# GNN layers: edges sorted on chip by target block, counts within the edge loop, target rows by one-hot products

## The chip, the cores and the metric

One core of one Trainium2 chip runs the whole program. The metric is device microseconds of one execution; the profile is of one further execution. Engines are named as in the profile: PE (TensorE), DVE (VectorE), ACT (ScalarE), POOL (GpSimd) and SP (SyncE).

## The reference, cut to what matters

625 nodes of 768 features, 20000 edges (src, dst). The reference is four blocks of a graph layer and a feed-forward or mixture layer. The part that changes is the first graph block, twice:

```python
fs = (x @ Ws + bs).reshape(-1, H, D)
fd = (x @ Wd + bd).reshape(-1, H, D)
e = jax.nn.leaky_relu(fs[src] + fd[dst], 0.2)
logits = jnp.einsum('ehd,hd->eh', e, attn)
m = jax.ops.segment_max(logits, dst, num_segments=N)
ex = jnp.exp(logits - m[dst])
denom = jax.ops.segment_sum(ex, dst, num_segments=N)
alpha = ex / denom[dst]
out = jax.ops.segment_sum(alpha[:, :, None] * fs[src], dst, num_segments=N)
```

H is 8 in the first layer and 1 in the second. A logit depends only on the pair (dst, src), so the kernel keeps a 625 x 625 table of logits and a 625 x 625 matrix of edge counts C, and forms the softmax densely with the logarithm of the counts added.

## The kernel before

The program is written by hand, engine by engine, with counted semaphores; each engine's order is that of its block of code. Stages are: layer norm and two linear layers (`linear`), first edge loop, attention over the table (`attend(0)`), two linear layers, second edge loop, `attend(1)`, then a mixture of 8 experts in units of up to 256 tokens (`mixture0`), and the later layers.

Nodes are split into T = 5 blocks of R = 125, edges into ET = 157 tiles of 128. The linear layers write rows of 776 floats (768 features, 8 linear terms), source rows by way of `F` to `src_rows`, target rows by way of `O` to `dst_rows` in DRAM (`edge_rows`, SP's `in_two`).

First edge loop, per tile: POOL issues an indirect gather of 128 source rows (L562) and of 128 target rows (L565) into one of EU = 8 buffer pairs, and six tiles later the indirect scatter of the 8 logits (L578), which waits for `s_lg` and for the landing of the scatter before. ACT copies each half of the target rows into PSUM (L1028); DVE adds the half of the source rows (L1377) and multiplies the positive part by the attention vector (L1379); then come the small sum of the linear terms (L1384), the sums per head (L1388) and the logit (L1412). Beside this the counts are built: DVE makes the one-hot of the targets (L1329, 626 columns, bf16 from fp16), ACT that of the sources (L1032, L1037), and PE adds their product into seven PSUM banks, eleven products a tile (L647, `count`).

Second edge loop, per tile: the same DMAs, scattering one logit into two tables in turn; ACT copies whole target rows into PSUM (L1048), DVE adds (L1393) and takes the whole product with its sum (L1397), then L1412. PE has no work. The loops of PE, ACT and DVE are `Fori` loops of eight tiles; POOL's is written out. `mixture0` is a `Fori` over at most NU = 12 units with an `If` inside; 8 units run, and PE reads a number of empty eighths (L875) and branches to one of five variants in each.

At the start SP loads x, then constants, then the edges; ACT's queue fills the logit tables (`zero_logits`).

## Time and profile before

| what | us |
|---|---|
| runs of the kernel | 3960.14, 3953.3, 3954.85 (median 3954.85) |
| the profiled execution, its own time | 3953.68 |
| its span, first to last instruction | 3951.8 |
| busy: PE / DVE / ACT / POOL | 2386.9 / 2330.5 / 1365.2 / 1002.3 |
| mean granted clock of PE | 0.770 of 2.4 GHz |

Busy time of an engine leaves out register, branch, semaphore and DMA-issuing instructions. A four-byte matmul has two records on PE. "Issue" as a releaser means that an engine waited for nothing the profile shows, "remote" that the release has no record.

### The profile page before, as it was taken

The numbers are of one execution on the slowest core, as the hardware profiler recorded it, in microseconds if no ns is written. First come the engines' busy times: TensorE is split into PE (matmuls) and PEld (weight loads), VectorE is DVE, ScalarE is ACT, GpSimd is POOL, SyncE is SP. The second block draws the span as 40 slices with busy tenths as digits, with TensorE's granted clock in tenths as the row PEclk, the third lists the DMA queues.
The fourth block names the chain that finished last, engine by engine and source line by source line (L and its number), as shares of the span: only waits on it lengthen the run. The fifth ranks groups of instructions, "written<-read, shape, count | busy, mean of one in ns | idle before, by whom it ended". The sixth has DMA issues, their size and how long they took to land.

```text
span 3951.8 us, 39567 instructions
## 1 busy us (share of the span) xinstructions
PE 2386.9 (60%) x12372; PEld 1922.0 (49%) x12373; DVE 2330.5 (59%) x4711; ACT 1365.2 (35%) x2102; POOL 1002.3 (25%) x1052
## 2 busy tenths in 40 slices
PE   8454455556700000034598988886788588797899
PEld 4243333345400000013588888775375345477798
DVE  4687777787344444435787776665575623576332
ACT  0455555554011111111465555553171101144110
POOL 0566666630176666631100000001000000000000
PEclk9766766677855555565799998988789698898899
DMA  9656565657376666630676555554200001100211
GB/s 283 186 168 181 169 175 173 175 167 280 97 193 187 191 190 189 187 103 1 221 252 204 204 200 186 184 181 149 80 1 12 21 17 37 60 13 25 72 72 43
DMA packets 118376, 546.25 MB, mean 138 GB/s; under 512 B 31254, under 2 KB 31510, under 8 KB 112904
## 3 DMA queue, kind: packets, MB, share of 16 engines
q0 software_dynamic: 69520, 283.95, 24.6%
q1 hardware_dynamic: 47142, 244.22, 18.5%
q10 hardware_dynamic: 1540, 15.63, 1.3%
q8 instruction: 126, 2.06, 0.2%
q14 instruction: 48, 0.39, 0.0%
HBM read 487.87 MB, written 55.82 MB: 138 GB/s over the span
## 4 chain that ended last, share of the span: by engine, by line
PE 43%; DVE 22%; issue 14%; POOL 7%; DMA 6%; ACT 4%; another core or an unknown queue 3%; DVEq 1%; SPq 0%; POOLq 0%; ACTq 0%
PE PS L678 10%; PE PS L931 6%; PE PS L830 5%; PE PS L733 5%; PE PS L845 4%; DVE PS L1377 4%; DVE WB L1379 3%; POOL WB L562 2%; PE PS L832 2%; POOL WB L565 2%; PE PS L848 2%; DVE WB L1397 2%; DVE W L1478 1%; PE PS L719 1%
## 5 line engine op out<-in xcount | busy, mean ns | idle before, releaser
L647 PE MATMUL PS<-O 128*125 128x512 bf16 (+9 forms) x1727 | 378.1, 390 | 355.7 <-ACT O L1037 260.4
L719 PE MATMUL PS<-ident,W 125*125 125x125 f32 x650 | 114.1, 313 | 747.8 <-issue 684.5
L647 PEld LDWEIGHTS PS<-O 128*125 128x125 bf16 x1727 | 261.6, 191 | 472.3 <-issue 306.1
L719 PEld LDWEIGHTS PS<-ident,W 125*125 125x125 f32 x650 | 95.4, 214 | 764.4 <-issue 706.1
L830 PE MATMUL PS<-urowsT,w1s 128*128 128x384 f32 (+4 forms) x1164 | 365.9, 382 | 94.1 <-issue 73.3
L678 PE MATMUL PS<-WB,XT 128*125 128x384 f32 (+1 forms) x1120 | 385.2, 507 | 31.9 <-DMA WB<-in_L_gnn_W 17.0
L562 POOL DMA_INDIRECT WB<-src_rows,idx x314 | 304.8, 971 | 288.4 <-DMA dst_rows<-O 193.3
L845 PE MATMUL PS<-hid,w2s 128*128 128x384 f32 (+3 forms) x1152 | 326.4, 357 | 0.5 <-DVE hid L1727 0.5
L678 PEld LDWEIGHTS PS<-WB,XT 128*125 128x125 f32 x1120 | 214.1, 192 | 200.0 <-issue 36.8
L733 PE MATMUL PS<-F,PT 125*125 125x96 f32 (+3 forms) x1500 | 292.6, 348 | 17.8 <-ACT PT L1103 8.2
L1048 ACT COPY PS<-WB 128x776 f32<-128x776 f32 x138 | 111.6, 809 | 551.5 <-DVE lgr L1412 367.9
L832 PE MATMUL PS<-urowsT,w1s 128*128 128x192 f32 (+4 forms) x1164 | 301.1, 259 | 0.0
L578 POOL DMA_INDIRECT logits<-lgr,key x236 | 233.9, 991 | 230.4 <-DVE lgr L1412 142.7
L550 POOL TENSOR_TENSOR rstd<-var,mhalf 125x1 f32<-125x1 f32 x50 | 41.5, 831 | 987.2 <-DVE var L1302 987.2
L830 PEld LDWEIGHTS PS<-urowsT,w1s 128*128 128x128 f32 x1164 | 233.6, 201 | 111.2 <-issue 91.2
L565 POOL DMA_INDIRECT WB<-dst_rows,idx x276 | 261.4, 947 | 85.2 <-issue 83.7
L848 PE MATMUL PS<-hid,w2s 128*128 128x192 f32 (+3 forms) x1152 | 282.3, 245 | 0.0
L1393 DVE TENSOR_TENSOR PS<-WB,PS 128x776 f32<-128x776 f32 x157 | 152.4, 971 | 219.9 <-ACT PS L1048 129.9
L931 PE MATMUL PS<-w3s,XT 128*128 128x384 f32 x1440 | 254.7, 339 | 11.1 <-DVE w3s L1792 11.1
L931 PEld LDWEIGHTS PS<-w3s,XT 128*128 128x128 f32 x1440 | 254.4, 189 | 12.3 <-issue 12.2
L733 PEld LDWEIGHTS PS<-F,PT 125*125 125x125 f32 x1500 | 230.5, 202 | 60.1 <-issue 17.2
L832 PEld LDWEIGHTS PS<-urowsT,w1s 128*128 128x128 f32 x1164 | 237.3, 204 | 0.0
(251 smaller groups left out, 4809.7 us busy)
## 6 DMA issues: line engine op xcount, KB each, us to landing
XN<-in_L_ffn_w SPq DMA_DIRECT2D x98, 769.0 KB, 4.4
PB<-in_L_ffn_w SPq DMA_DIRECT2D x97, 768.0 KB, 5.6
logits<-NEG ACTq DMA_DIRECT2D x8, 1367.2 KB
WB<-logits SPq DMA_DIRECT2D x5, 2187.5 KB
slot_rows<-WB POOLq DMA_DIRECT2D x13, 768.0 KB, 29.6
slot_outs<-WB POOLq DMA_DIRECT2D x12, 768.0 KB, 54.5
C<-in_L_ffn_expert_w SPq DMA_DIRECT2D x8, 1152.0 KB, 5.6
NEG<-in_L_ffn_expert_w SPq DMA_DIRECT2D x8, 1152.0 KB, 6.8
```

Source lines behind the costliest of these rows:

```text
L562: pool.indirect_dma_start(out=gs[u], out_offset=None, in_=src_rows, in_offset=bass.IndirectOffsetOnAxis(ap=idx[:, i, 0:1], axis=0)).then_i ...
L565: pool.indirect_dma_start(out=gd[u], out_offset=None, in_=dst_rows, in_offset=bass.IndirectOffsetOnAxis(ap=idx[:, i, 1:2], axis=0)).then_i ...
L578: pool.indirect_dma_start(out=table, out_offset=bass.IndirectOffsetOnAxis(ap=key[:, i:i + 1], axis=0), in_=lgr[:, i % EU, 0:HEADS[g]["h"]] ...
L647: mm = pe.matmul(PSz[0:R, a:b], oh[:, slot, 1, c * R:(c + 1) * R], oh[:, slot, 0, a - c * N:b - c * N], start=(first and fresh), stop=last ...
L678: mm = pe.matmul(PS[0:R, 4 + g % 4, 0:hw], XT[:, k, t * R:(t + 1) * R], w[:, k, half * hw:(half + 1) * hw], start=(k == 0), stop=(k == kc ...
L719: tr = pe.transpose(PSz[0:R, 1024 * (1 + s % 2) + b * P:1024 * (1 + s % 2) + b * P + R], src[:, b * R:(b + 1) * R], ident[0:R, 0:R])
L733: mm = pe.matmul(PS[0:R, bank, 0:cw], PT[0:R, s % 2, b, :], F[0:R, b, col:col + cw], start=(b == 0), stop=(b == T - 1))
L830: pe.matmul(both(q % 2, columns), w1s[:, g % 2, 0, w:w + P], urowsT2[:, :, k * TU:k * TU + columns], start=k == 0, stop=False)
L832: mm = pe.matmul(PS[:, q % 2, 0:columns], w1s[:, g % 2, 1, w:w + P], urowsT2[:, 0, k * TU:k * TU + columns], start=False, stop=k == KD - 1)
L845: pe.matmul(both(2 + k, columns), w2s[:, g % 2, 0, w:w + P], hid2[:, g % 2, :, c * TU:c * TU + columns], start=g == 0 and c == 0, stop=False)
L848: mm = pe.matmul(PS[:, 2 + k, 0:columns], w2s[:, g % 2, 1, w:w + P], hid2[:, g % 2, 0, c * TU:c * TU + columns], start=False, stop=g == NG ...
L931: mm = pe.matmul(PS[:, 4 + 2 * ((MB3 + d) % 2) + half, 0:384], XT2[:, a, k, t * R:t * R + P], w3s[:, 2 * u + k // 3, b, col:col + 384], st ...
```

## The change

- Ahead of the first layer norm DVE counts, for each edge, its place in an order by target block (`rank_edges`: comparisons, a prefix sum in eight steps, two small products on PE for the sums over partitions). Each block starts a new tile, so there are ES = 161 tiles, the rest padded.
- The edges are moved on PE between the pieces of the two linear layers (`move_edges`): the product of a one-hot of the place within a tile (ACT, `place_onehots`) and of the place's tile times the node numbers (DVE, `edge_values`), in groups of NB = 16.
- All edges of a tile now have targets in one block. Their target rows are no longer gathered from DRAM: PE multiplies the turned one-hot of the targets (128 edges from 125 nodes) with that block's rows in `O` and adds to source rows that ACT copied into PSUM. `dst_rows` and its writes are gone. The turned one-hots come from the target numbers, turned once, stored to DRAM and spread over all partitions by DMA in chunks of 16 tiles (`spread_targets`).
- A tile's counts touch one block: two products in place of eleven, banks 0 to 4 and the last 113 columns in banks 5 and 6. The long one-hot is made by DVE for even tiles, by ACT for odd ones. PE reads the tile's block number into a register (`block`).
- The second loop uses the same sum on PE. All edge loops and the units of `mixture0` are written out instead of `Fori`.
- Edges, iota and ident are loaded ahead of x; the table fills go to SP's queue; POOL does the two large memsets.

```diff
+ES = (E + T * (P - 1)) // P
+NB = 16
...
-        zh = PS[:, 7, 0:D // 2]
-        zw = [PSz[:, 1024 * b:1024 * b + GW] for b in range(4)]
+        zw = [PS[:, 2 * b:2 * b + 2, 0:GW // 2] for b in range(4)]
+        zA = PS[:, 6, P - 15:P - 15 + HA]
+        zB = PS[:, 7, 0:GW - HA]
+        rest = PSz[0:R, 5 * 512:5 * 512 + T * P].rearrange("p (c n) -> p c n", c=T)[:, :, 0:N - 512]
...
+            def spread_targets(g):
+                chunks = -(-ES // CH)
+                sp.wait_ge(s_frow, 2 * T * (g + 1))
+                for c in range(chunks):
+                    q = g * chunks + c
+                    if c >= 2:
+                        sp.wait_ge(s_tt, ES * g + CH * (c - 1))
+                    a, b = CH * c, min(CH * (c + 1), ES)
+                    sp.dma_start(spread_ids[q % 2][:, 0:(b - a) * P],
+                                 targets[a:b].rearrange("(o t) p -> o (t p)", o=1).to_broadcast([P, (b - a) * P]))\
+                      .then_inc(s_idb[q % 2], 16)
...
-                pool.indirect_dma_start(
-                    out=gd[u], out_offset=None, in_=dst_rows,
-                    in_offset=bass.IndirectOffsetOnAxis(ap=idx[:, i, 1:2], axis=0)).then_inc(s_gat[u], 16)
+                    in_offset=bass.IndirectOffsetOnAxis(ap=source[:, i:i + 1], axis=0)).then_inc(s_gat[u], 16)
...
+            def move_edges(a, b):
+                pe.wait_ge(s_trc, 2 * T)
+                for t in range(a, min(b, ET)):
+                    pe.wait_ge(s_q, t + 1)
+                    pe.wait_ge(s_val, t + 1)
+                    pe.matmul(PS[:, 0, 0:2 * ES], ohq[t % NB], ohv[t % NB], start=t == 0, stop=t == ET - 1)\
+                      .then_inc(s_pm, 1)
...
+            def first_edges():
+                pe.wait_ge(s_line, 2 * T * 2)
+                pe.wait_ge(s_zero, 1)
+                for bank in (2, 3, 4, 5, 6, 7, 0, 1):
+                    if bank == 1:
+                        pe.wait_ge(s_idc, 1)
+                    mm = pe.matmul(PS[:, bank, :], NEG[:, 0, 0:P], iota[:, 0:512], start=True, stop=False,
+                                   skip_group_check=True)
+                mm.then_inc(s_seed, 1)
+                pe.wait_ge(s_frow, 2 * T)
+                c, then = block(0), block(1)
+                for i in range(ES):
+                    wait(pe, s_wa, i)
+                    pe.wait_ge(s_oh, i + 1)
+                    if i % 2:
+                        pe.wait_ge(s_ohs, i // 2 + 1)
+                    pe.matmul(rest[:, bass.ds(c, 1), :].rearrange("p o n -> p (o n)"), oht[i % 4][:, 0:R],
+                              ohs[i % 4][:, 512:N], start=False, stop=i == ES - 1, skip_group_check=True)\
+                      .then_inc(s_rem, 1)
+                    pe.matmul(PS[0:R, bass.ds(c, 1), :].rearrange("p o n -> p (o n)"), oht[i % 4][:, 0:R],
+                              ohs[i % 4][:, 0:512], start=False, stop=i == ES - 1, skip_group_check=True)\
+                      .then_inc(s_ohu, 1)
+                    pe.wait_ge(s_tt, i + 1)
+                    pe.wait_ge(s_ca, i + 1)
+                    pe.matmul(zA, ohT[i % 2], O[0:R, bass.ds(c, 1), 0:HA].rearrange("p o n -> p (o n)"),
+                              start=False, stop=True, skip_group_check=True).then_inc(s_za, 1)
+                    pe.wait_ge(s_gc, i + 1)
+                    pe.matmul(zB, ohT[i % 2], O[0:R, bass.ds(c, 1), HA:GW].rearrange("p o n -> p (o n)"),
+                              start=False, stop=True, skip_group_check=True).then_inc(s_zp, 1)
+                    c, then = then, block(i + 2) if i + 2 < ES else None
...
+            linear(0, lambda t: move_edges(NB * (t - 1), NB * t) if t else None)
+            linear(1, lambda t: move_edges(NB * (T + t - 1), NB * (T + t)))
+            move_edges(NB * (2 * T - 1), ET)
+            turn_targets()
+            first_edges()
...
-                with pe.Fori(1, NU) as u:
-                    with pe.If(u < units):
+                for u in range(1, NU):
+                    with pe.If(units > u):
...
+            def place_onehots(a, b):
+                def place_gap(t):
+                    wait(act, s_q, t - 1)
+                    act.activation(qgap[t % 2], iota16[:, 0:P], ACT.Abs, bias=place_in[:, t:t + 1], scale=-1.0)\
+                       .then_inc(s_qg, 1)
+                if a == 0:
+                    act.wait_ge(s_place, 1)
+                    place_gap(0)
+                for t in range(a, b):
+                    if t + 1 < ET:
+                        place_gap(t + 1)
+                    act.wait_ge(s_qg, t + 1)
+                    wait(act, s_pm, t - NB + 1)
+                    act.activation(ohq[t % NB], qgap[t % 2], ACT.Relu, bias=ones[:, 0:1], scale=-1.0).then_inc(s_q, 1)
...
+            def edge_values(a, b):
+                for t in range(a, min(b, ET)):
+                    wait(dve, s_pm, t - NB + 1)
+                    dve.tensor_scalar(ohv[t % NB][:, 0:ES], iota16[:, 0:ES], tile_of[:, t:t + 1], dst1[:, t:t + 1],
+                                      ALU.is_equal, ALU.mult)
+                    dve.tensor_scalar(ohv[t % NB][:, ES:2 * ES], iota16[:, 0:ES], tile_of[:, t:t + 1],
+                                      src1[:, t:t + 1], ALU.is_equal, ALU.mult).then_inc(s_val, 1)
...
+                for i in range(2):
+                    count_onehots(i)
+                    turned_onehot(0, i)
+                for i in range(ES):
+                    weigh_first(i)
+                    if i:
+                        head_sums(i - 1)
+                    if i + 2 < ES:
+                        count_onehots(i + 2)
+                    weigh_last(i)
+                    if i + 2 < ES:
+                        turned_onehot(0, i + 2)
+                    if i:
+                        finish(i - 1)
...
+            pool.memset(NEG[:], 0.0).then_inc(s_zero, 1)
+            pool.memset(C[:], NEGBIG).then_inc(s_low, 1)
```

The order on DVE, first edge loop, one tile before (`gs`, `gd` and the products are in WB, PS is PSUM, PB holds the attention vector):

```order
L1377 TENSOR_TENSOR PS<-WB,PS 128x384
L1379 SCALAR_TENSOR_TENSOR WB<-PS,PB 128x384
L1329 TENSOR_SCALAR O<-XT,idf 128x626
L1377 TENSOR_TENSOR PS<-WB,PS 128x384
L1379 SCALAR_TENSOR_TENSOR WB<-PS,PB 128x384
L1384 TENSOR_TENSOR WB<-WB 128x8
L1388 TENSOR_REDUCE dots<-WB 128x8
L1412 SCALAR_TENSOR_TENSOR lgr<-dots,WB 128x8
```

and now, for a tile in which the long one-hot is DVE's:

```order
L1633 SCALAR_TENSOR_TENSOR WB<-PS,WB 128x392
L1646 TENSOR_REDUCE dots<-WB 128x8
L1573 TENSOR_SCALAR O<-XT,idf 128x125
L1575 TENSOR_SCALAR W<-XT,idf 128x626
L1639 COPY F<-PS 128x8
L1640 SCALAR_TENSOR_TENSOR WB<-PS,WB 128x384
L1625 TENSOR_SCALAR WB<-WB,node 125x128
L1653 SCALAR_TENSOR_TENSOR lgr<-dots,F 128x8
```

The two additions are gone; the short one-hot, the tail copy and the turned one-hot are new; the long one-hot is in every second tile.

The order on PE, first edge loop, one tile now (before it was eleven L647 products of 53 to 512 columns and nothing else):

```order
L747 TENSOR_LOAD idx
L747 ISA x2
L766 ISA
L766 MATMUL PS<-W,O 125x113
L769 ISA
L769 MATMUL PS<-W,O 125x512
L774 ISA
L774 MATMUL PS<-O,WB 128x392
L777 ISA
L777 MATMUL PS<-O,WB 128x384
```

Counts first, then the two four-byte products of the target rows; the rows ISA and TENSOR_LOAD set registers.

The order on PE in the linear layers, before:

```order
L662 MATMUL PS<-ident,XN 128x125 x30
L678 MATMUL PS<-WB,XT 125x384 x120
```

and now, one of its nine rounds:

```order
L827 MATMUL PS<-WB,XT 125x384 x12
L737 MATMUL PS<-W,O 128x322 x9
L737 MATMUL PS<-PT,O 128x322 x6
L737 MATMUL PS<-PT,F 128x322
```

After each twelve products of a linear layer (from the second on) sixteen tiles of edges are moved.

## Rows read from the trace of the kernel before

**Rows 1.** Engines by stage: PE, PEld, DVE, ACT, POOL busy us, clock, DMA.

```profile
0.00:108.00 108.00, 84.77 (x270) 51.17 (x271) 46.72 (x78) 6.02 (x11) 4.25 (x9) 1.00 0.87 266
108.00:840.00 732.00, 378.07 (x1727) 261.64 (x1727) 556.69 (x1258) 390.57 (x629) 456.40 (x471) 0.67 0.59 171
...
1068.00:1727.00 659.00, 0.00 (x0) 0.00 (x0) 313.15 (x628) 127.02 (x157) 455.64 (x470) 0.50 0.67 189
```

**Rows 2.** First edge loop, groups by form: out<-in, shapes xcount | busy us, mean ns | idle.

```profile
L1377 DVE TENSOR_TENSOR PS<-WB,PS 128x384 f32<-128x384 f32 x310 | 172.9, 558 | 26.2 <-issue 13.5 <-ACT PS L1028 12.2
L1379 DVE SCALAR_TENSOR_TENSOR WB<-PS,PB 128x384 f32<-128x384 f32 x310 | 172.7, 557 | 10.7
L578 POOL DMA_INDIRECT logits<-lgr,key x154 | 152.1, 988 | 170.3 <-DVE lgr L1412 99.3 <-issue 63.7 <-DMA logits<-lgr,key 7.3
L562 POOL DMA_INDIRECT WB<-src_rows,idx x152 | 147.5, 971 | 46.3 <-issue 46.3
L1388 DVE TENSOR_REDUCE dots<-WB 128x8 f32<-128x768 f32 x154 | 146.8, 953 | 0.0
L1028 ACT COPY PS<-WB 128x384 f32<-128x384 f32 x271 | 130.8, 483 | 193.8 <-DVE WB L1379 148.6 <-issue 45.2
L565 POOL DMA_INDIRECT WB<-dst_rows,idx x134 | 127.0, 947 | 41.9 <-issue 40.4 <-DMA logits<-lgr,key 1.5
L1037 ACT ACTIVATE O<-XT,ones 128x626 bf16<-128x626 bf16 x155 | 126.1, 814 | 104.7 <-remote 99.7 <-PE PS L647 5.0
...
L1329 DVE TENSOR_SCALAR O<-XT,idf 128x626 bf16<-128x626 f16 x155 | 61.2, 395 | 128.2 <-remote 118.5 <-PE PS L647 9.4
...
L1412 DVE SCALAR_TENSOR_TENSOR lgr<-dots,WB 128x8 f32<-128x8 f32 x154 | 24.2, 157 | 0.0
```

**Rows 3.** First edge loop, in order of time: start us, us, what [idle before <-releaser].

```profile
553.40 0.39 DVE L1329 TENSOR_SCALAR O<-XT,idf 128x626 bf16<-128x626 f16 x1 [4.69 <-remote]
...
554.31 2.91 PE L647 MATMUL PS<-O 128*125 128x512 bf16 x11 [6.45 <-ACT O L1037]
...
562.21 1.56 PE L647 MATMUL PS<-O 128*125 128x512 bf16 x11 [0.93 <-ACT O L1037]
```

**Rows 4.** Waits of the first edge loop: us in total, times, longest us.

```profile
DVE O L1329 <- remote: 118.5, 33, 6.3
```

**Rows 5.** Second edge loop, groups by form, columns as in rows 2.

```profile
L1393 DVE TENSOR_TENSOR PS<-WB,PS 128x776 f32<-128x776 f32 x147 | 142.7, 971 | 202.8 <-ACT PS L1048 114.0 <-issue 88.8
L562 POOL DMA_INDIRECT WB<-src_rows,idx x147 | 142.6, 970 | 44.8 <-issue 44.8
L1397 DVE SCALAR_TENSOR_TENSOR WB<-PS,PB 128x768 f32<-128x768 f32 x147 | 139.9, 952 | 6.5 <-DVE PS L1393 5.4 <-issue 1.1
```

**Rows 6.** First and last start of one line in each loop.

```profile
L1377 DVE TENSOR_TENSOR PS<-WB,PS x314: 543/555/564, 116.1 to 832.7; 128x384 f32<-128x384 f32 x157
...
L1393 DVE TENSOR_TENSOR PS<-WB,PS x157: 970/971/972, 1073.8 to 1718.8; 128x776 f32<-128x776 f32 x157
```

**Rows 7.** Start of the program, in order of time, columns as in rows 3.

```profile
12.18 1.02 DVE L1299 BATCH_NORM_STATS2 stats<-X 125x6 f32<-125x384 f32 x2 [4.49 <-DMA X<-in_x]
...
24.69 77.97 PE L678 MATMUL PS<-WB,XT 128*125 128x384 f32 x240
...
108.27 1.19 POOL L562 DMA_INDIRECT WB<-src_rows,idx  x1 [86.82 <-DMA dst_rows<-O]
```

**Rows 8.** A short activation, group by form on ACT, whole span.

```profile
L1155 ACT ACTIVATE F<-F 128x256 f32<-128x256 f32 x192 | 77.7, 415 | 51.2 <-DVE F L1717 50.0
```

**Rows 9.** DMA issues of the page: KB each, median us to landing.

```profile
XN<-in_L_ffn_w SPq DMA_DIRECT2D x98, 769.0 KB, 4.4
```

**Rows 10.** Seams of mixture units on PE, in order of time, columns as in rows 3.

```profile
2104.85 0.68 PE L830 MATMUL PS<-urowsT,w1s 128*128 128x384 f32 x1 [10.81 <-issue]
...
2202.19 0.74 PE L830 MATMUL PS<-urowsT,w1s 128*128 128x448 f32 x1 [5.80 <-issue]
```

**Rows 11.** Waits of PE from unit 1 to the last, columns as in rows 4.

```profile
PE PS L830 <- issue: 71.9, 6, 16.3
```

More of the change, by code:

```diff
@@ L623, in _ @@
             unit_store(0)
-            with pool.Fori(1, NU) as u:
-                with pool.If(u < units):
+            for u in range(1, NU):
+                with pool.If(units > u):
                     unit_store(u)
@@ new lines, in second_edges @@
+            def second_edges():
+                pe.wait_ge(s_line, 2 * T * 4)
+                for bank in range(8):
+                    mm = pe.matmul(PS[:, bank, 0:GW // 2], ones[:], iota[:, 0:GW // 2], start=True, stop=False,
+                                   skip_group_check=True)
+                mm.then_inc(s_seed, 1)
+                pe.wait_ge(s_frow, 4 * T)
+                c, then = block(0), block(1)
+                for i in range(ES):
+                    pe.wait_ge(s_tt, ES + i + 1)
+                    pe.wait_ge(s_gc, ES + i + 1)
+                    for half in range(2):
+                        mm = pe.matmul(zw[i % 4][:, half, :], ohT[i % 2],
+                                       O[0:R, bass.ds(c, 1), half * (GW // 2):(half + 1) * (GW // 2)]
+                                       .rearrange("p o n -> p (o n)"), start=False, stop=True, skip_group_check=True)
+                    mm.then_inc(s_zp, 1)
+                    c, then = then, block(i + 2) if i + 2 < ES else None
@@ L680, in linear @@
                         mm.then_inc(s_linp, 1)
-            def count_edges():
-                for i in range(EU):
-                    count(i, i % 2, first=i == 0)
-                with pe.Fori(1, ER) as j:
-                    for u in range(EU):
-                        count(j * EU + u, u % 2)
-                for i in range(ER * EU, ET):
-                    count(i, i % 2, last=i == ET - 1)
-                pe.wait_ge(s_cnt, 1)
+                    if between:
+                        between(t)
             def attend(n):
@@ L1187, in mixture0 @@
                 unit(0)
-                with act.Fori(1, NU) as u:
-                    with act.If(u < units):
+                for u in range(1, NU):
+                    with act.If(units > u):
                         unit(u)
@@ L1764, in mixture0 @@
                 unit(0)
-                with dve.Fori(1, NU) as u:
-                    with dve.If(u < units):
+                for u in range(1, NU):
+                    with dve.If(units > u):
                         unit(u)
```

519 lines of the change are left out of this document (323 added, 196 removed).

## The prediction

> **What bounds the kernel now.** I read the stages first, then the groups of the two edge loops, then waits and order of time where these left a question.
>
> The two edge loops last 732 and 659 us of the 3951.8 us span, over a third [rows 1]. In the first, DVE is busy 557 us and POOL 456 us, PE's mean clock is 0.67 of full; in the second PE does nothing at all. The reader should see that POOL's busy time hides a gap after each of its DMAs: "issue" before the 152 source gathers is 46.3 us, 0.30 us each [rows 2]. With it a first-loop tile costs POOL 0.97 + 0.95 + 0.99 + 3 x 0.30 = 3.81 us. DVE spends 2 x 0.558 + 2 x 0.557 + 0.953 + 0.395 and two small operations of 0.157 = 3.89 us, partly overlapped [rows 2]. Undisturbed tiles follow each other every 3.83 us: DVE and POOL bind together. The stage is longer, because DVE waits 33 times, 118.5 us in all, at its one-hot for a release no record explains [rows 4]. Such a stall is at 553.40: DVE and PE stop together, PE resumes at half clock (2.91 us for a tile's eleven count products) and is back at full (1.56 us) two tiles later [rows 3]. I can't name its cause, only that PE ran at full clock with idle time in each tile before it. From first to last product the loop takes 116.1 to 832.7, the second 1073.8 to 1718.8 [rows 6]: 717 and 645 us, 4.6 and 4.1 us per step.
>
> **The change, part by part.**
>
> Front. The sort stands ahead of the layer norm on DVE: some 75 operations. From the two forms of 384 and 776 columns (0.558 and 0.971 us [rows 2, 5]) an operation costs 0.153 us + 1.07 ns per column; about 11,000 columns and 75 starts give 23 us, and 17 if the two-byte ones run at double rate, as L1329 does (626 columns in 0.395 us). I take 20. It starts when edges, iota and ident have landed, now ahead of x. X was there at 12.18 [rows 7]; I take 6, so the places are ready at 26. Then ACT makes 16 place one-hots before it copies transposed rows. An activation of 128 columns is, by the line through 0.415 us for 256 and 0.814 us for 626 [rows 2, 8], 0.28 us, so a pair is 0.57 us and the sixteen 9 us. Ten copies of about 0.6 us follow: the linears start at 42 in place of 24.69 [rows 7]. Their 240 records take 78 us. Between them PE moves 157 tiles; a count product averages 284 columns in 1.56/11 = 0.14 us [rows 3], so 322 columns are about 0.18 us, 28 us on PE's path. ACT needs 16 x 0.57 = 9.1 us per batch against PE's 7.8 + 2.9, DVE 16 x 2 x 0.24 = 7.7 us beside some 3 us of row work: both just hidden; were PE faster, ACT would be next. The linears and moves end at 148, sorted_edges (nine short operations) at 152. The old first gather, at 108.27, waited for dst_rows [rows 7]; that wait goes. In its place comes a chain: turn on PE, copy on ACT, store, spread, one-hot. A DMA of 769 KB lands in 4.4 us [rows 9]; two in a row are 4 to 9 us, I take 7, with PE and ACT 9. PE's eight opening products of 512 columns, 8 x 0.87 = 7 us, lie beside that chain (before the second loop 5 us beside its first gather). SP's 20 table fills moved ahead of the row stores, and POOL's two memsets ahead of its roots: both have over 100 and 15 us of cover; without it the tables (15.6 MB) would hold the source rows back by tens of us. First product at 161 for 116.1: **+45 us**, between +25 and +75.
>
> First loop, DVE: products of 392 and 384 columns 0.566 + 0.557; head sums 0.953; short one-hot 0.14 (125 columns, by L1329's rate); the long one every second tile 0.20; tail copy 0.12 to 0.157; turned one-hot of 128 columns, two-byte in, four-byte out, 0.14 to 0.29, taken 0.20; finish 0.157. Sum 2.9 us. POOL: one gather and one scatter, 0.97 + 0.99 + 0.60 = 2.56 us. ACT: 2 x 0.49, and 1.63/2 = 1.8 us. PE, at full clock: a four-byte product of 384 columns is two records of 0.325 us [rows 7], so 0.66 + 0.65, counts 0.27, and up to 0.2 for weights not loaded ahead, since each product stands behind a wait: about 2.0 us. The chain that closes through PE: rest product, ACT's copy, first 392 columns, DVE's first product; with 0.05 to 0.15 us per handover 2.4 us at full clock, shorter than DVE's. At half clock PE's own order decides: 1.5 + 1.4 (the two products) + 0.3 (rest) + 0.65 (ACT's copy and handovers) = 3.9 us. So 3.0 at full, 3.9 at half. The old loop's mean of 0.67 [rows 1] means full clock for a third of its time; PE will be busy for two thirds of a tile at full clock where it was for 1.56 of 3.83 us, so I choose 70% at full, between a third and all: 3.25 us. 161 x 3.25 = 523 for 717: **-194 us**. Reading the block number into a PE register and four computed addresses per tile cost, by no row here, anything from nothing (PE's sequencer works ahead) up to the 5.80 us of a seam [rows 10]; each mixture unit reads one too, and of the seven seams only six have a gap [rows 11], so I take nothing and keep the upper end for a rival.
>
> Second loop: DVE 0.97 (weigh, add moved to PE) + 0.08 + 0.20 + 0.157 = 1.4 us, ACT 0.81, POOL 2.56, PE 1.3 to 1.5 us at full and 2.7 to 2.9 at half clock. POOL's 2.56 and a PE that drifts between clocks give 2.6 to 2.9; the old loop ran 8% over POOL's 3.81; I take 2.75, 443 for 645: **-202 us**. Its start gains about 6 us: the gather no longer waits for the target rows to land, though SP's spread takes part of that place. **-6 us**.
>
> Mixture units. The loop over units becomes straight code. At six seams PE idles 71.9 us on "issue" [rows 11]: the shortest, 5.80, I read as the jump back, the longer (10.81 to 16.3) as that and jumps into a column variant [rows 10]. The latter stay. 6 x 5.8 = 35 us go; four skipped units now are far jumps on DVE ahead of the last gathers, 4 x 5.8 less what POOL's last store hides, about 10 us. **-25 us**, between 0 and -60. The Trainium skill, Runtime: NRT & Kernel Launch, "Instruction fetch mechanics", says that a taken branch out of the current window must fetch its target before going on. By that rule even the skipped units cost a fetch each; the gaps of 5.80 and 10.81 us agree with it.
>
> Sum: 45 - 194 - 202 - 6 - 25 = -382. Against the profiled execution's own 3953.7 us that is 3571; attend(1) finds PE warm and its first sums (idle PE before) some 2 us faster. I say **3570 us**. The median of the runs shown lies 1.2 us above that execution: no difference here.
>
> A rule against the change. L562 gathers take 0.971 us in the first loop, where DVE runs its two-byte one-hot at double rate, and 0.970 in the second, where it doesn't [rows 2, 5]: no interference visible, and I charge none. The Trainium skill, SBUF — State Buffer, "Who interferes with whom", says that tensor_scalar in such modes takes the ports that GpSimd needs, and the other blocks. By that rule the new two-byte operations (0.5 us per first-loop tile, 0.2 per second-loop tile) could stretch POOL's 2.56 to 3.1 and 2.8. That would change nothing in the first loop and add some 8 us to the second.
>
> **The rivals.** A measurement of this kernel tells changes from about 0.2% on.
>
> *PE sets the first loop's pace.* It stays at half clock, or the unexplained stalls come back with their 0.75 us per tile. For it: PE had them in this very loop, and it now stands inside the chain. Against: PE is busier. 161 x (3.9 - 3.25) = +105, with stalls +120 to 150; about 3690 us.
>
> *Scatter landings set it.* Each first-loop scatter waits until the one before has landed. That wait was free under 3.83 us; landing plus 0.99 + 0.3 us may be over 3.25. For it: scatters queue behind gathers. Against: half the gather bytes are gone. If the pace stays 3.83, +93: 3665 us.
>
> *All covers hold.* Clock full throughout, 3.0 and 2.6 us per tile, front +35: -40 - 24 - 10: about 3495 us.
>
> *Slower than before.* The register read and the computed addresses sit between a wait and its product, unhidden, and PE starves to half clock. The change has 382 us to lose over 322 tiles, so it decides from 1.2 us more per tile in both loops, mean 4.2. At 2 us per tile on top of the half-clock chains (5.9 and 4.8 us) it is 161 x (2.65 + 2.05) = +757: about 4330 us. For it: nothing but the missing price. Against: the seventh seam, which reads such a value without a gap.
>
> *The counts or the sort don't shorten anything*, since only the gathers' halving frees POOL: DVE would remain at 3.8. Against: the rows show which DVE operations leave. I include it in the second rival.
>
> **How the numbers follow.** Forecast 0.50, its own range 3500 to 3640; PE's pace 0.27; scatter 0.06; all covers 0.13; slower 0.04. The range 3460 to 3730 holds the first four but for their outer ends. Faster by over 0.2% takes all but the last: 0.95; within 0.01; slower 0.04.
>
> **What would show it.** First product near 161; step of the first loop near 3.0 where PE's product has full duration, 3.9 where double; POOL idle there, and busy without pause at 2.6 us in the second; linears 106 us long with the moves; seams without 5.8. Wrong: POOL's scatter waiting on its own landing, PE's idle time on "issue" inside the loops, or DVE waiting again for an unexplained release.

## The result, and the profile after

The changed kernel took **3661.36 us**, median of 4 runs (3653.06 to 3670.72), beside 3955.98 us for the kernel before (4 runs, 3953.3 to 3960.14): ratio 0.9255, 95% interval 0.9228 to 0.9282. The forecast was 3570 us, its range 3460 to 3730. The sign is right. The time lies 91 us above the likeliest value and outside the forecast's own range of 3500 to 3640; it is inside the wide range, close to the 3665 of the rival "scatter landings". The profiled execution took 3656.48 us, 297 us less than the one of before. By stage (each boundary is the start of the same operation in both traces):

| stage | forecast | measured |
|---|---|---|
| start to first product of the first loop | +45 | 116.1 to 171.6: +55.5 |
| first loop, first to last product | -194 | 716.6 to 526.1: -190.5 |
| to the first linear behind it | 0 | +6.7 |
| linears to the first product of the second loop | -6 | -3.5 |
| second loop, first to last product | -202 | 645.0 to 490.0: -155.0 |
| to the first scatter into slot_rows | -2 | 161.8 to 188.8: +27.0 |
| mixture's units, to the first gather behind them | -25 | 859.5 to 822.1: -37.4 |
| rest | 0 | +0.1 |

The windows of the changed kernel show the stages that answer to [rows 1] (columns: PE, PEld, DVE, ACT, POOL busy us, clock, DMA share, GB/s):

```profile
70.00:150.00 80.00, 71.52 (x277) 40.39 (x275) 75.89 (x268) 76.42 (x221) 0.00 (x0) 1.00 0.25 64
150.00:171.60 21.60, 15.57 (x33) 5.78 (x33) 6.75 (x30) 11.72 (x28) 7.03 (x7) 0.68 0.42 139
171.60:697.70 526.10, 396.92 (x961) 147.47 (x962) 407.88 (x1196) 258.14 (x476) 305.43 (x310) 0.94 0.46 128
942.00:1432.00 490.00, 307.97 (x640) 142.10 (x640) 199.66 (x638) 128.80 (x160) 306.44 (x313) 0.75 0.57 137
```

The old first loop had a clock of 0.67, the new one 0.94. POOL is busy 305 of 526 us in the first loop. In the second it should work without pause (306 us busy and 0.30 us behind each of its 322 DMAs, 403 us), but the loop lasts 490. What ends the waits there (us in total, times, longest), first loop:

```profile
DVE WB L1633 <- PE PS L774: 104.6, 133, 3.8
POOL logits L659 <- issue: 95.2, 117, 1.6
POOL logits L659 <- DMA logits<-lgr,key: 45.3, 21, 3.6
POOL logits L659 <- DVE lgr L1653: 31.3, 18, 8.4
```

and second loop:

```profile
DVE WB L1687 <- remote: 150.5, 29, 7.9
DVE WB L1687 <- PE PS L795: 92.6, 63, 15.1
POOL logits L659 <- DMA logits<-lgr,key: 26.8, 4, 17.8
```

No "remote" wait is left in the first loop ([rows 4] had 118.5 us of them). The long ones stand in the second loop now, where the old kernel did nothing on PE and DVE had 16.1 us of such waits in all, none over 2.3 us. One of them in order of time:

```profile
1211.15 1.56 PE L795 MATMUL PS<-O,WB 125*128 x4 [1.07 <-ACT PS L1228]
...
1216.10 0.97 DVE L1687 SCALAR_TENSOR_TENSOR WB<-PS,WB 128x776 f32<-128x776 f32 x1 [5.79 <-remote]
...
1217.41 2.95 PE L795 MATMUL PS<-O,WB 125*128 x4 [4.70 <-DVE WB L1625]
```

By its records PE had finished at 1212.7 (1211.15 + 1.56); DVE was let go at 1216.1, and PE's next four records run at half clock (2.95 us for 1.56), just as in [rows 3].

The second new thing is a wait of POOL, here in order of time on POOL alone:

```profile
1241.98 0.99 POOL L659 DMA_INDIRECT logits<-lgr,key  x1 [0.30 <-issue]
1243.27 0.97 POOL L646 DMA_INDIRECT WB<-src_rows,idx  x1 [0.30 <-issue]
1244.55 0.99 POOL L659 DMA_INDIRECT other<-lgr,key  x1 [0.30 <-issue]
1245.85 0.97 POOL L646 DMA_INDIRECT WB<-src_rows,idx  x1 [0.30 <-issue]
1264.67 0.99 POOL L659 DMA_INDIRECT logits<-lgr,key  x1 [17.85 <-DMA logits<-lgr,key]
```

Scatter 102 waits until scatter 100, issued at 1241.98, has landed, some 22 us later. The forecast knew of no such landing. What is special in tile 100 is the padding of the sort: the inputs have 9032, 3716, 2771, 2374 and 2107 edges in the five target blocks, so the tiles that end a block (70, 100, 122, 141, 158) have 56, 124, 45, 58 and 69 padded slots (71 x 128 - 9032 = 56), and tiles 159 and 160 nothing else. All padded slots have one key, N*N: each scatter writes them to one address. Behind the loop the same shows as DVE's wait for the tables, 20.0 us in the kernel before:

```profile
DVE W L1734 <- DMA WB<-other: 48.6, 1, 48.6
```

### The profile page after: what moved, and what is told of

It reads as the page before. It is cut to its first block, busy times and chain, and to the rows that moved or that the text cites. A ratio compares the mean times of both kernels' runs of the same rounds, so it can differ in the third digit from the quotient of the medians.

```text
span 3654.7 us, 39491 instructions
## 1 busy us (share of the span) xinstructions
PE 2755.0 (75%) x12450; PEld 1968.3 (54%) x12450; DVE 2166.5 (59%) x5061; ACT 1350.1 (37%) x2276; POOL 729.6 (20%) x756
## 4 chain that ended last, share of the span: by engine, by line
PE 49%; issue 14%; DVE 13%; POOL 9%; DMA 9%; ACT 4%; another core or an unknown queue 1%; SPq 0%; POOLq 0%; ACTq 0%; DVEq 0%
PE PS L827 10%; PE PS L1072 7%; PE PS L971 6%; PE PS L874 5%; POOL WB L646 5%; PE PS L986 5%; POOL logits L659 3%; DMA logits<-lgr,key 3%; PE PS L973 3%; PE PS L989 2%; DVE W L1736 1%; PE PS L860 1%; DMA WB<-src_rows,idx 1%; PE PS L774 1%; DMA other<-lgr,key 1%
## 5 line engine op out<-in xcount | busy, mean ns | idle before, releaser
L795 PE MATMUL PS<-O,WB 125*128 x644 | 310.4, 631 | 184.5 <-DVE WB L1625 89.1
L646 POOL DMA_INDIRECT WB<-src_rows,idx x322 | 314.4, 976 | 328.4 <-DVE idf L1567 126.7
L795 PEld LDWEIGHTS PS<-O,WB 125*128 125x128 f32 x644 | 142.9, 240 | 352.0 <-issue 322.1
L1687 DVE SCALAR_TENSOR_TENSOR WB<-PS,WB 128x776 f32<-128x776 f32 x161 | 155.5, 966 | 292.8 <-remote 150.5
L1228 ACT COPY PS<-WB 128x776 f32<-128x776 f32 x161 | 130.3, 810 | 459.5 <-DMA WB<-src_rows,idx 164.7
L659 POOL DMA_INDIRECT logits<-lgr,key x242 | 242.7, 1003 | 270.9 <-issue 116.1
L774 PE MATMUL PS<-O,WB 125*128 x322 | 159.9, 581 | 112.3 <-ACT PS L1211 85.3
L989 PEld LDWEIGHTS PS<-hid,w2s 128*128 128x128 f32 x1152 | 220.2, 191 | 0.0
L986 PEld LDWEIGHTS PS<-hid,w2s 128*128 128x128 f32 x1152 | 216.6, 188 | 4.7 <-issue 0.6
```

What stands on the lines that cost most here:

```text
L646: pool.indirect_dma_start(out=gs[u], out_offset=None, in_=src_rows, in_offset=bass.IndirectOffsetOnAxis(ap=source[:, i:i + 1], axis=0)).th ...
L659: pool.indirect_dma_start(out=table, out_offset=bass.IndirectOffsetOnAxis(ap=key[:, i:i + 1], axis=0), in_=lgr[:, i % EU, 0:HEADS[g]["h"]] ...
L774: pe.matmul(zA, ohT[i % 2], O[0:R, bass.ds(c, 1), 0:HA].rearrange("p o n -> p (o n)"), start=False, stop=True, skip_group_check=True).then ...
L795: mm = pe.matmul(zw[i % 4][:, half, :], ohT[i % 2], O[0:R, bass.ds(c, 1), half * (GW // 2):(half + 1) * (GW // 2)] .rearrange("p o n -> p ...
L986: pe.matmul(both(2 + k, columns), w2s[:, g % 2, 0, w:w + P], hid2[:, g % 2, :, c * TU:c * TU + columns], start=g == 0 and c == 0, stop=False)
L989: mm = pe.matmul(PS[:, 2 + k, 0:columns], w2s[:, g % 2, 1, w:w + P], hid2[:, g % 2, 0, c * TU:c * TU + columns], start=False, stop=g == NG ...
```

## The experiments

The experiments ran on three chips, of which the kernel before needs 3821 to 3823 us on one (e1 to e8) and 3973 to 3976 us on the others (e9 to e12, e13). So times are compared within one chip.

**Padding.** Theory: the writes of padded slots to one address land slowly. Rival: the reads of one source row, or nothing to do with padding.

e1:

```diff
-                dve.tensor_scalar(pad, idf[:, 1, :], 0.0, float(N * N + N + 1), ALU.is_lt, ALU.mult)
+                link(dve.tensor_scalar(tally[:, 5, 0:1], node[:], 16.0, float(N * N + N + 1), ALU.mult, ALU.add))
+                dve.tensor_scalar(pad, idf[:, 1, :], 0.0, tally[:, 5, 0:1], ALU.is_lt, ALU.mult)
```

> Edit: each padded slot of a sorted tile scatters to a dump row of its own (64 bytes apart), where the changed kernel sends all of them to one row; they still gather source row 0. The two wholly padded tiles at the end and the tiles that end a target block (56, 124, 45, 58, 69 padded slots) are where the changed kernel's second loop stands still. Theory (many 4-byte writes to one address land slowly, about 0.16 us each): the second loop loses its pauses of 8, 20 and 9 us before scatters 72, 103 and 143, 20 to 30 us in all, and the load of the tables behind it comes some 28 us earlier (DVE's wait for it back from 48.6 to about 20 us): 3661 - 50 = about 3610 us. The first loop, with 32-byte rows, gains less than 5. Rival (the pauses come from 128 reads of one source row, or have nothing to do with padding): within 10 us of 3661, pauses where they were.

e2 (behind e1's edit):

```diff
-                dve.tensor_scalar(inside, idf[:, 0, :], 0.0, None, ALU.max)
+                link(dve.tensor_scalar(tally[:, 4, 0:1], node[:], 1.0, None, ALU.add))
+                link(dve.tensor_scalar(inside, idf[:, 1, :], 0.0, tally[:, 4, 0:1], ALU.is_lt, ALU.mult))
+                link(dve.tensor_tensor(inside, inside, idf[:, 0, :], ALU.add))
```

> Edit: as e1, and each padded slot also gathers a source row of its own instead of row 0. Theory (the writes): within 5 us of e1. Rival (the reads of one row): e1 stays near 3661 and this one is some 50 us faster. If both matter, e1 gains a part and this one the rest.

To size them, the changed kernel ran on the same chip:

> The changed kernel itself, unedited, beside the next three on one chip, since the kernel before took 3821 us where e1, e2 and e4 ran and 3956 where the changed kernel was first measured. If the pauses that no record explains (150 us of DVE's waits in the second loop) belong to the chip, this run shows hardly any of them, its second loop lasts about 450 us (2.8 a tile) for 490, and it takes about 3600 to 3610 us; if they belong to the kernel, 3660 and 150 us of them. The ratio to before should be 0.925 to 0.945 either way.

Measured: changed kernel 3616.64 us (4 runs), e1 3549.77 (4), e2 3547.69 (4; the 2 us between them are within the scatter of the runs). The writes are the cause and the reads are not: **-67 us**, more than the 50 expected. Of it the second loop has 34 us (first and last start of the weigh operation: duration ns, then from, to), e5 first:

```profile
L1687 DVE SCALAR_TENSOR_TENSOR WB<-PS,WB x161: 966/967/968, 941.6 to 1389.4; 128x776 f32<-128x776 f32 x161
```

```profile
L1688 DVE SCALAR_TENSOR_TENSOR WB<-PS,WB x161: 966/967/968, 939.7 to 1353.9; 128x776 f32<-128x776 f32 x161
```

2.80 us a tile, and 2.59 without the pile-up: that is POOL's 0.97 + 0.99 + 2 x 0.30 = 2.56 [rows 2], nothing else in the way. Another 30 us lie behind the loop (189.1 us to the first scatter into slot_rows in e5, 159.3 in e1), where e1's DVE waits 19.4 us for the tables:

```profile
DVE W L1735 <- DMA WB<-other: 19.4, 1, 19.4
```

By the semaphore events of e5, from a scatter's issue to its landing: 9.8 us with 56 padded slots, 20.9 with 124, 20.0 and 20.3 with 128. The same tiles land in 3.0, 3.0, 2.1 and 2.1 us in e1, so a write to one address costs 0.12 to 0.14 us (0.10 with 45 slots, 9.0 for 4.4 us). The scatter behind such a one is late as well: tile 101 has no padding, goes to the other table and still lands after 22.0 us. In the first loop, with rows of 32 bytes instead of 4, the padded tiles of e5 land in 2.1 to 3.3 us, beside a median of 2.4 for all: there the same repetition costs next to nothing. The Trainium skill, DMA: Bandwidth & Descriptors, "Rules for kernel authors", says that destination indices must be unique within one scatter, since each duplicate's write goes out on its own and one lands. What the repetition costs in time is this trace's.

e12, the same with `node[:], 1.0` for `node[:], 16.0`:

> Edit: e1 with the dump rows of the padded slots 4 bytes apart in the second layer's tables (16 of them in 64 bytes), not 64. Theory (only writes to the very same address queue up): the scatters of padded tiles land as in e1, in 1 to 7 us, and the total is e1's within 10 us. Rival (writes within 64 bytes queue up too): landings of 10 to 20 us where 124 or 128 slots are padded, and the changed kernel's time comes back in part, +20 to +67 us.

3616.48 us (2 runs) beside 3973.49, ratio 0.9098; e9 below, with rows 64 bytes apart (and e4's order in the first loop), has 0.9078 on that chip. The second loop's step is 2.96 and 2.93 us. In the totals the two can hardly be told apart, but the landings can. The load of the tables waits for the landing of scatter 160, which has 128 padded slots. e12, scatter and load:

```profile
1419.62 0.97 POOL L659 DMA_INDIRECT logits<-lgr,key  x1 [2.71 <-DMA logits<-lgr,key]
1427.62 0.86 SPq L453 DMA_DIRECT2D WB<-logits  x2
```

and e9:

```profile
1415.57 0.97 POOL L659 DMA_INDIRECT logits<-lgr,key  x1 [0.64 <-issue]
1417.73 0.86 SPq L453 DMA_DIRECT2D WB<-logits  x2
```

8.0 us with rows 4 bytes apart, 2.2 with 64, and 20.3 in e5 with all in one: neighbours within 64 bytes still cost about 0.05 us a write (an estimate, 5.8 us over 128), a third of what one address costs. DVE's wait for the tables is 28.8 us in e12, 20.0 in e9. So e12 came out between its theory (landings of 1 to 7 us) and its rival (10 to 20).

**What sets the first loop's pace.** I first took a chain through PE, ACT and DVE for it. e4 puts the count products of tile i+1 ahead of the second product of tile i, and takes them away where they stood:

```diff
                     pe.matmul(zA, ohT[i % 2], O[0:R, bass.ds(c, 1), 0:HA].rearrange("p o n -> p (o n)"),
                               start=False, stop=True, skip_group_check=True).then_inc(s_za, 1)
+                    if i + 1 < ES:
+                        counts(i + 1, then)
                     pe.wait_ge(s_gc, i + 1)
```

> Edit: in the first loop PE does the two count products of tile i+1 ahead of the second product of tile i, not behind it. Theory (the step of 3.29 us is set by a chain through PE, ACT and DVE: weigh_last, ACT's second copy, PE's second product, the count products, ACT's first copy, PE's first product, weigh_first, which two steps share): the order takes the second product out of it, DVE's idle time before its first product (118 us) mostly goes: 3.29 to 2.7 or 2.9 us a tile, -60 to -95 us, about 3585. Rival (DVE's own operations, 3.14 us a tile by their durations one after the other, bind): less than 20 us. Rival 2 (the clock falls more, since PE idles more per tile): no gain or slower.

3607.45 us (4 runs), 9 less than e5 (ratios to before 0.9449 and 0.9454, no difference clear of the noise), the step 3.28 us as before: the theory fell. DVE's waits for PE, 118.9 us ahead of one operation in e5, are 49.9 and 49.4 us ahead of two, and no more. POOL's own timeline in e5 shows why:

```profile
300.89 0.98 POOL L659 DMA_INDIRECT logits<-lgr,key  x1 [0.64 <-issue]
302.18 0.97 POOL L646 DMA_INDIRECT WB<-src_rows,idx  x1 [0.30 <-issue]
304.18 0.98 POOL L659 DMA_INDIRECT logits<-lgr,key  x1 [1.03 <-DMA logits<-lgr,key]
305.47 0.97 POOL L646 DMA_INDIRECT WB<-src_rows,idx  x1 [0.30 <-issue]
308.12 0.98 POOL L659 DMA_INDIRECT logits<-lgr,key  x1 [1.68 <-DVE lgr L1653]
```

Each scatter waits for the landing of the one before. By the semaphore events of e5 the landing comes 2.54 us after the issue began (2.10 at best), and the next scatter starts 0.80 us behind it (0.775 both at the 5th and at the 95th percentile): 3.34 us on the mean, which is the step but for the ends of the loop. At the median the scatter starts 9.6 us after DVE had begun the operation that makes its logits. The label "DVE lgr" on such a wait is wrong: DVE was done long before. Two runs took the wait away; in both, half of the first layer's logits go to a table that nothing reads, so they size the wait and are no kernels to use.

e6:

```diff
-                    wait(pool, s_sc, 16 * i)
-                    table, done = logits8, s_sc
+                    wait(pool, s_sc[i % 2], 16 * (i // 2))
+                    table, done = (logits8, other8)[i % 2], s_sc[i % 2]
```

> Edit: the first loop's scatters go in turn to logits8 and to a second table that nothing reads, each with its own semaphore, so that a scatter waits for the landing of the one before the last; half of the first layer's logits are left out of what attend reads. Theory (the first loop is paced by POOL: each scatter's issue, 0.98 us, its landing, 1.5 us, and 0.78 us until POOL has gone on): the step falls from 3.28 us to the next bound, between POOL's 2.57 and 2.95 us, so -55 to -110 us in that loop. Rival (DVE's operations or the chain through PE and ACT set the step): within 0.08 us of 3.28.

> Edit: that of e6 and that of e4 together (half of the first layer's logits are left out). If behind the landings the chain through weigh_last, ACT's second copy and PE's second product is the next bound, this one is 0.1 to 0.3 us per tile faster than e6; if DVE's own operations or POOL's 2.57 us are, both have the same step within 0.05 us.

e6 took 3577.69 us (2 runs), e7 3544.65 (2). From first to last product (e5 526.1 us), of e6:

```profile
L1635 DVE SCALAR_TENSOR_TENSOR WB<-PS,WB x161: 566/567/568, 171.1 to 660.9; 128x392 f32<-128x392 f32 x161
```

and e7:

```profile
L1641 DVE SCALAR_TENSOR_TENSOR WB<-PS,WB x161: 566/567/568, 170.9 to 624.1; 128x392 f32<-128x392 f32 x161
```

3.29, 3.06 and 2.83 us a tile: the landings bind first, the chain that e4's order shortens second. The clock was 1.00 in both runs and 0.95 in e5, so a part of e6's gain may be PE's. What is left at 2.83 is mostly DVE: it is busy for 415 of e7's 453 us (2.59 a tile), and these are all of its waits:

```profile
DVE F L1647 <- PE PS L785: 31.7, 86, 1.0
DVE WB L1641 <- PE PS L780: 3.4, 2, 3.3
```

**The seams.** e8, on all five engines:

```diff
-                for u in range(1, NU):
-                    with pe.If(units > u):
+                with pe.Fori(1, NU) as u:
+                    with pe.If(u < units):
```

> Edit: the mixture's units are a loop of the hardware again on all engines, as before the change. Theory (each of six seams costs PE a jump back of 5.8 us, less about 10 us for skipped units): 25 to 40 us more than the changed kernel on the same chip, PE's idle time on issue ahead of its first product of a unit back from 52 to 72 us. Rival (the seams cost nothing, the mixture's -37 us came from elsewhere, such as its start or the clock): within 10 us.

3662.08 us (4 runs), 45 more than e5. PE's waits in the units, of e8:

```profile
PE PS L971 <- issue: 87.5, 7, 18.5
```

and of e5:

```profile
PE PS L971 <- issue: 51.1, 13, 10.7
```

36 of the 45 us stand in these two rows. The rival fell. What is left in e5, 51 us in 13 gaps of up to 10.7, has 44 us at the six seams, where straight code can only jump forward; no run took those jumps away.

**The unexplained releases.** e5 has none: all of its DVE waits in the second loop end with PE.

```profile
DVE WB L1687 <- PE PS L795: 250.9, 150, 21.9
```

So they depend on the chip as well as on the loop. The name misleads: "remote" means that the release has no record, and the traces that have such waits lack many records. The changed kernel's holds 18,716 semaphore events, e5's 25,097 for the same program; e9's, e11's and e12's hold 18,400 to 18,700. The stall itself is real, since PE's own records pause for 4.70 us in the lines above, but nothing says that a foreign engine released DVE. Nor is a falling clock enough: in the second loop it fell 20 times in the changed kernel's trace and 22 times in e5's, which has none of these waits. e9 met them again; it is e1 and e4 together:

> Edit: e1 and e4 together. e1 took 67 us less than the changed kernel beside the same kernel before (3549.8 and 3616.6), e4 9 us less. Theory (two separate terms, and the landings in logits8 still pace the first loop): 3535 to 3545 us where before takes 3822, ratio 0.926. Rival (with the order of e4 the first loop gains more once padding no longer disturbs it): under 3530.

3611.00 us (5 runs) beside 3973.49, ratio 0.9078 (0.9063 to 0.9093). The expectation in us was for the other chip and can't be read here; its ratio of 0.926 was missed, as the ratios differ between chips too (0.9454 and 0.9255 for the changed kernel). The second loop takes 2.93 us a tile where e1 took 2.59, with the waits back:

```profile
DVE WB L1694 <- remote: 136.8, 32, 7.3
```

e11, which is e1 with filler products on PE, tested whether they come from PE idling at full clock:

```diff
                     pe.wait_ge(s_gc, ES + i + 1)
+                    for half in range(2):
+                        pe.matmul(PS[:, 2 * (i % 4) + half, GW // 2:512], ones[:], iota[:, 0:512 - GW // 2],
+                                  start=False, stop=True, skip_group_check=True)
```

> Edit: e1, and PE does two products of 124 columns more per tile in the second loop, ahead of its two and into the same banks' unused columns. Where this runs on a chip with the pauses that no record explains, theory (they need PE idle at full clock): the clock of that stage goes from 0.75 to over 0.95 and the pauses mostly go. Where it runs on one without them, both theories say that POOL's 2.57 us per tile stays the pace: the loop within 0.1 us a tile of e1's 2.59, total within 10 us of e1; if PE has become part of the chain, 2.7 to 3.0 a tile, +15 to +65 us.

3621.68 us (4 runs), same chip as e9. Windows of the second loop, e9 and e11:

```profile
943.10:1413.40 470.30, 309.81 (x640) 144.79 (x640) 200.58 (x639) 129.51 (x160) 307.00 (x313) 0.75 0.51 143
```

```profile
938.20:1426.30 488.10, 355.42 (x1280) 226.30 (x1280) 200.83 (x641) 129.02 (x160) 306.29 (x313) 0.84 0.49 137
```

and e11's waits:

```profile
DVE WB L1691 <- remote: 139.0, 33, 6.7
```

The clock rose only to 0.84 and the waits are all there: 33 for 32 (e12, the nearest run without filler on that chip, had 23, 98.0 us). As far as the filler went, the theory got no support; it missed its own 0.95, so it isn't excluded for a PE that never idles.

**The front, and a version of all gains.** e10 gives POOL every fourth place one-hot:

```diff
+            for t in range(3, ET, 4):
+                wait(pool, s_pm, t - NB + 1)
+                pool.tensor_scalar(ohq[t % NB], iota16[:, 0:P], place_in[:, t:t + 1], None, ALU.is_equal)\
+                    .then_inc(s_qp, 1)
```

> Edit: e9, and POOL makes every fourth place one-hot of the sort (is_equal on 128 two-byte columns), ACT the other three. Theory (a batch of sixteen moves between two rounds of the linears lasts 11.65 us because ACT's two activations take 0.72 us per tile, 16 x 0.72 = 11.5): ACT then needs 12 x 0.72 = 8.7, PE's 7.8 + 16 x 0.18 = 10.7 binds, and the first product of the first loop comes at 160 to 165 in place of 171: -6 to -10 us against e9. Rival (PE or DVE bind as closely, or POOL's operations hold up DVE's two-byte ones): less than 3 us, or slower.

First product at 163.5 for e9's 171.4, as expected; the total, 3605.37 (5 runs), is 6 us less, ratio 0.9063 (0.9047 to 0.9079), which these runs can't tell from e9's. Of the 7.9 us in the front the linears' start has 2.6 (36.2 for 38.8), the rounds 5.3.

e13 gives the two tables of e6 a complete form:

```diff
+                                both = ltile[:, t % 2].rearrange("p n h -> p (n h)")
+                                dve.tensor_tensor(both, both, XTz[0:R, 0:8 * N], ALU.max).then_inc(s_mx8, 1)
```

> Edit: e10, and the first loop scatters to two tables in turn as in e6, but nothing is left out: both tables are filled with the low value (12.5 MB more), each tile of logits of both is loaded, and DVE takes the larger of the two (five operations of 5000 columns, about 5.3 us each). Theory: the first loop's step goes from 3.29 to e7's 2.83 us, -73 us; of the new work the 26 us on DVE and the second loads lie mostly beside attend's other work, +5 to +25 us in that stage; the longer fill holds the source rows back by nothing to 10 us. Against e10 -40 to -70 us: ratio to before 0.888 to 0.896 on a chip where before takes about 3973, 0.905 to 0.915 where it takes 3822. Rival (the second load and the joining stand in attend's path, or the fill reaches into the first loop): -20 us or less.

3620.22 us (5 runs) beside 3976.49, ratio 0.9095 (0.9067 to 0.9124): the rival won. There is no gain over e10 (0.9047 to 0.9079), and since the intervals touch, no loss that these runs show for sure. Windows of e13, the first loop and attend behind it, then e10's:

```profile
164.20:665.80 501.60, 353.68 (x960) 151.55 (x960) 416.12 (x1197) 272.18 (x475) 313.31 (x312) 0.93 0.47 135
665.80:858.90 193.10, 90.82 (x633) 85.81 (x633) 143.84 (x303) 74.37 (x139) 21.04 (x33) 0.70 0.80 257
```

```profile
163.50:689.80 526.30, 368.33 (x961) 155.59 (x961) 421.60 (x1197) 267.57 (x476) 304.42 (x310) 0.90 0.46 128
689.80:844.10 154.30, 85.65 (x633) 77.00 (x633) 116.20 (x298) 72.96 (x138) 26.07 (x35) 0.75 0.70 241
```

Attend pays 39 us for the second loads and the joining, which stand in its path (DVE is busy there 28 us more and waits 22.8 us for the second table, where e10 waits 16.2 for the first); the loop gains 25, not 73: 3.13 us a tile, at a clock of 0.93 where e7 had 1.00. It ran on a third chip, so how much of the difference to e7 is the chip wasn't separated.

## Why the prediction was right, and where not

**The total came within the wide range in part by luck.** The first loop's number came out by another mechanism than the forecast's, and the second loop and the way behind it took 74 us more than it said, for padding and stalls that it didn't have.

**Front, +45, was +55.5.** The start of the linears (39 for 42) was 3 us better. "ACT needs 16 x 0.57 = 9.1 us per batch against PE's 7.8 + 2.9" was mis-sized. The changed kernel's groups between 70 and 150 us:

```profile
L1174 ACT ACTIVATE F<-XT,F 128x128 f16<-128x128 f16 x111 | 44.7, 403 | 3.6
L1185 ACT ACTIVATE O<-F,ones 128x128 f16<-128x128 f16 x103 | 39.9, 387 | 0.0
```

Not 0.28 us each but 0.40 and 0.39. A tile's pair takes 0.72 us (two overlap a little), 16 of them 11.5, and a round took 11.65 us: ACT, busy 76 of 80 us in the window above, was the bound, not PE. Nine rounds of 0.95 us more are 8.6 us, and e10 gave most of them back. The last 13 tiles, behind the linears, went at ACT's pace too: the moves ended at 157.3 for 148, which makes 4 us more, and the way from there to the first product took 14.3 us for 13. Two points, 256 and 626 columns, were no line to extend down to 128. (The line for DVE's operations has a small slip too: its two rows give 1.05 ns per column, not 1.07; nothing hangs on it.)

**First loop, -194, was -190.5: the number by luck, the reason wrong.** The step was forecast at 3.25 from 3.0 at full and 3.9 at half clock with PE at full for 70% (which gives 3.27). It was 3.29, but the clock was 0.94, and e6 and e4 show that scatter landings set the pace. That was the rival with 0.06. The forecast dismissed it since "half the gather bytes are gone", and priced it at the old pace of 3.83; it had no row for a scatter's landing. The term that failed is this wait, put at nothing: issue to landing 2.54 and 0.80 until the next scatter. The trace of before could have warned of it. It has nine waits of a scatter for the landing before it, 9.2 us in all. Here is one, with the scatter ahead of it:

```profile
155.29 0.98 POOL L578 DMA_INDIRECT logits<-lgr,key  x1 [0.35 <-issue]
...
159.69 0.99 POOL L578 DMA_INDIRECT logits<-lgr,key  x1 [0.89 <-DMA logits<-lgr,key]
```

4.40 us from one to the next, over the old pace of 3.83 and well over the forecast's 3.25. The next bound was near the forecast's: 2.83 in e7 at full clock for 3.0. Its parts were less so: the eight operations of a tile last 3.10 us one by one in e7, for 2.91 in the sum (the short one-hot 0.25 for 0.14, the turned one 0.28 for 0.20), but they overlap to 2.59.

**Second loop, -202, was -155.** On e5's chip the step was 2.80 us, for 2.75 forecast, but of two parts that weren't in it as such: 2.59 by POOL (forecast 2.56 at least) and 0.21 for the padded slots, which the forecast didn't see at all, though the changed kernel's code gives all of them one key. On the first chip 0.26 us more: the unexplained releases, 29 waits. The rival "PE sets the first loop's pace" priced their return, at 0.75 us per tile, but in the wrong loop.

**Behind the second loop, -2, was +27.** Not a term of the sum. It is the padding again: two scatters of 128 writes to one address, ahead of the tables' load (e1: 29.8 us back).

**Mixture, -25, was -37.4.** Two terms were off. "About 10" for the skipped units was nothing: from PE's last product of the units to the first gather it is 10.5 us before and 10.0 after. And the seams gave less than 35: the six gaps are 11.7, 4.6, 4.8, 4.4, 9.8 and 9.8 us, 45.1 in all for 71.9 [rows 11], so 27 us went. Two of them, and all of PE's such waits:

```profile
1842.78 0.66 PE L971 MATMUL PS<-urowsT,w1s 128*128 128x384 f32 x1 [11.65 <-issue]
...
1938.12 0.71 PE L971 MATMUL PS<-urowsT,w1s 128*128 128x448 f32 x1 [4.58 <-issue]
```

```profile
PE PS L971 <- issue: 51.8, 13, 11.7
```

Another 6 us are PE's own products (703.2 us busy for 708.9, at a clock of 0.93 for 0.91), 3 the way to the first of them. On e5's chip e8 prices the whole at 45 us. The Trainium skill's rule on taken branches (Runtime: NRT & Kernel Launch, "Instruction fetch mechanics") was cited for seams that stay; the gaps left at all six agree with it.

**The slower rival** fell entirely: register reads and four computed addresses per tile leave no idle time that a step of 2.59 (e1) or 2.83 us (e7) could hold. **The rule against the change** (the Trainium skill, SBUF — State Buffer, "Who interferes with whom") didn't show: POOL's gathers take the same in the first loop, where DVE runs two-byte one-hots, as in the second. That is no test of the rule itself, which is about modes that use both ports: no run shows whether these one-hots run in such a mode.

```profile
L646 POOL DMA_INDIRECT WB<-src_rows,idx x154 | 150.4, 977 | 50.1 <-issue 48.2 <-DMA logits<-lgr,key 1.9
...
L646 POOL DMA_INDIRECT WB<-src_rows,idx x154 | 149.9, 973 | 48.5 <-issue 45.5 <-DMA other<-lgr,key 1.9 <-DMA logits<-lgr,key 1.2
```

The sum gives 3953.7 - 382 = 3571.7 us, and the profiled execution took 84.8 more: front 10.5, first loop 3.5, the ways to the two next stages 6.7 and 2.5, second loop 47, behind it 27, mixture -12.4, which add up to it. The 47 of the second loop are 34 of padding (447.8 - 414.2, e5 and e1), 42 of unexplained releases (490.0 - 447.8) and -29, since POOL's bare pace makes 414.2 us and not 443. The padding is the largest single term that was missing, 63 us in both places. The quickest version that computes everything is e10, 0.9063 of before where the changed kernel's ratio, on another chip like it, is 0.9255.

**Open.** The 6.7 us behind the first loop weren't looked into. What the "remote" releases are: the long ones come with some chips and not with another, in one loop and hardly in its neighbour, and more work on PE doesn't drive them out. Their traces lack records, and whether the recording itself has a part in the stalls was not tested. Whether the chips differ by anything else, the runs don't say; there was no trace of the kernel before on the quick one. That the 152 us by which it is quicker there are its 33 stalls is an inference.

## What to carry to other kernels

Work that fills a hole with "harmless" entries has a price of its own: give padded entries different addresses, and not neighbouring ones, above all in scatters of 4-byte rows. When a change takes work off an engine that issues DMAs one behind the other's landing, add up issue, landing and restart first; that loop may be the next bound however idle the engine looks. And two bounds that close on each other must be removed together: the order of e4 gained nothing clear alone and 0.23 us a tile once the landings were out of the way.

## What the runs showed of the hardware that was not expected

- A scatter of 128 slots, 4-byte rows, issue to landing: 20.0 to 20.3 us when all go to one address (e5), 8.0 when they lie 4 bytes apart (e12, tile 160), 2.1 when 64 bytes apart (e1, e9). With 56 of the slots at one address 9.8, with 124 20.9. With rows of 32 bytes 2.1 to 3.3, even to one address (e5).
- Such a scatter holds up the one behind it: 22.0 us for tile 101 of e5, which has no padding and another table.
- A short two-byte activation on ACT (128 columns) takes 0.39 to 0.40 us, hardly less than 0.415 for 256 [rows 8].
- The same kernel differs by 4% between chips (3823 and 3973 us), and a change by 2 points of its ratio (0.9454, 0.9431 to 0.9478, in e5; 0.9255 before it).
- The waits labelled "remote" stand in traces that hold 16,200 to 18,700 semaphore events; the traces of the quick chip hold 25,100 and have none.
- In waits that end with a scatter's landing the profile often names another releaser ("issue", or an operation that ended 10 us earlier).
